# Two cross-attention layers on one core: the last batch's image values weighed by a TensorE product with a block-diagonal matrix

## The reference, cut to what matters

```python
probs_ip = jax.nn.softmax(fused, axis=-1)                 # b h s 4
probs_ip = probs_ip * spatial_mask[None, None, :, None]
ip_out = jnp.einsum('bhsn,bhnd->bhsd', probs_ip, v_ip)    # 4 image values per head
ip_out = ip_out.transpose(0, 2, 1, 3).reshape(B, S, C)
out = text_out + IP_SCALE * ip_out                        # IP_SCALE = 1
out = out @ W_out + b_out
out = out + residual
```

## Time and profile before

| | |
|---|---|
| runs | 1620.91, 1628.34, 1626.88 us, median 1626.88 |
| profiled execution | 1620.88 us, of which the span of its instructions is 1619.1 us |
| PE busy | 1521.6 us, 94% of the span |
| DVE busy | 1270.9 us, 78% |
| ACT busy | 1051.9 us, 65% |
| POOL busy | 421.7 us, 26% |
| granted TensorE clock, mean | 0.983 |

### The profile page before, as it was taken

One profiled execution on the slowest core, in us unless ns is written; L12 is line 12 of the kernel. 1 busy time (PEld: TensorE's weight loads), 2 busy tenths in 40 slices (PEclk: granted clock), 3 DMA queues, 4 the chain that ended last, 5 costly groups with the idle time before them and its releaser, 6 DMA issues.

```text
span 1619.1 us, 24966 instructions
## 1 busy us (share of the span) xinstructions
PE 1521.6 (94%) x7536; PEld 1154.4 (71%) x7536; DVE 1270.9 (78%) x3537; ACT 1051.9 (65%) x2243; POOL 421.7 (26%) x993
## 2 busy tenths in 40 slices
PE   6899999999999999999999999999999999999993
PEld 3565389999656549999856637999965654899991
DVE  2598379998779738999779945999977983799985
ACT  1598267776269737777529936777725982777760
POOL 0244022222034302322104412222302440232220
PEclk9899999999999999999999999999999999999996
DMA  9211321111411132111131123111140113111110
GB/s 300 62 45 22 107 58 21 21 21 23 127 26 43 44 95 63 25 21 17 47 103 40 36 76 101 21 21 21 19 136 16 45 37 107 16 26 21 21 18 16
DMA packets 160222, 84.50 MB, mean 52 GB/s; under 512 B 121925, under 2 KB 130901, under 8 KB 160089
## 3 DMA queue, kind: packets, MB, share of 16 engines
q1 hardware_dynamic: 157448, 77.80, 19.5%
q10 hardware_dynamic: 2640, 5.11, 0.9%
HBM read 41.78 MB, written 34.10 MB: 47 GB/s over the span
## 4 chain that ended last, share of the span: by engine, by line
PE 85%; ACT 6%; issue 3%; SPq 2%; DVE 2%; DMA 1%; DVEq 0%; ACTq 0%
PE ps_w L1029 50%; PE ps_s L1029 16%; PE ps_t L1029 12%; PE ps_b L1029 5%; ACT probs L591 3%; PE ps_b L1154 2%; ACT probsT_high L572 1%; ACT probsT L580 1%; DMA slots<-out_all 1%; DVE row_max L802 1%; SPq L373 1%; SPq L325 0%; DMA slots<-probsT_low 0%; ACT probs L677 0%; PE ps_m L1029 0%
## 5 line engine op out<-in xcount | busy, mean ns | idle before, releaser
L572 ACT ACTIVATE probsT_high<-ps_t 128x512 fp32r<-128x512 f32 x640 | 385.1, 602 | 95.9 <-PE ps_t L1029 92.7
L787 DVE TENSOR_TENSOR probsT_low<-probsT,probsT_high 128x512 fp32r<-128x512 f32 x560 | 378.9, 686 | 17.3 <-ACT probsT L580 12.0
L580 ACT ACTIVATE probsT<-ps_t 128x512 f32<-128x512 f32 x640 | 388.2, 606 | 0.0
L1029 PE MATMUL ps_w<-gram,probsT_high 128*128 128x416 f32 (+2 forms) x1280 | 383.9, 310 | 1.1 <-issue 1.1
L1029 PE MATMUL ps_w<-gram_low,probsT_high 128*128 128x384 f32 (+2 forms) x1280 | 351.5, 303 | 0.0
L606 ACT ACTIVATE probs<-ps_s,row_max 128x508 f32<-128x508 f32 x320 | 222.5, 696 | 145.9 <-DVE row_max L852 105.5
L1029 PE MATMUL ps_s<-slots 96*128 96x512 f32 x640 | 280.6, 481 | 23.9 <-DVE row_max L802 9.3
L1029 PE MATMUL ps_t<-slots 98*128 98x512 f32 x640 | 251.6, 413 | 1.1 <-ACT probsT L580 0.2
L1029 PEld LDWEIGHTS ps_w<-gram_low,probsT_high 128*128 128x128 f32 (+1 forms) x1280 | 241.9, 189 | 6.3
L1029 PE MATMUL ps_w<-gram,probsT_low 128*128 128x400 f32 (+2 forms) x1280 | 245.9, 314 | 0.0
L1029 PEld LDWEIGHTS ps_w<-gram,probsT_high 128*128 128x128 f32 (+1 forms) x1280 | 240.4, 188 | 6.1 <-issue 1.8
(11 more groups left out here) (175 smaller groups left out, 1854.1 us busy)
## 6 DMA issues: line engine op xcount, KB each, us to landing
slots<-parts SPq DMA_DIRECT2D x128, 192.0 KB, 3.4
slots<-row_max SPq DMA_DIRECT2D x640, 0.5 KB, 2.0
parts<-probsT_high SPq DMA_DIRECT2D x16, 512.0 KB, 4.2
parts<-probsT_high SPq DMA_DIRECT2D x24, 256.0 KB, 4.1
parts<-probsT_low SPq DMA_DIRECT2D x8, 512.0 KB, 3.6
parts<-x_sb SPq DMA_DIRECT2D x8, 512.0 KB, 3.9
slots<-probsT_high SPq DMA_DIRECT2D x24, 128.0 KB, 3.3
parts<-probsT_low SPq DMA_DIRECT2D x12, 256.0 KB, 3.6
```

The costliest lines, as they stand in the source:

```text
L572: nc.scalar.activation(probsT_high[1 - par][:, t, :], ps_t[:, t % 2, :], ACT.Exp, scale=scale)
L580: nc.scalar.activation(probsT[:, t, :], ps_t[:, t % 2, :], ACT.Exp, scale=scale).then_inc(pt_block[l], 1)
L787: nc.vector.tensor_tensor(probsT_low[1 - par][:, t, :], probsT[:, t, :], probsT_high[1 - par][:, t, :].bitcast(F32), ALU.subtract).then_in ...
L1029: return nc.tensor.matmul(out, lhsT, rhs, start=start, stop=stop)
```

## The change

In the last batch alone, VectorE no longer weighs the image values. It writes the text part of the heads straight to the place that is transposed, in four products (one a chunk), and releases `heads_ready` there. It then normalizes the image weights in four products of 128x80 into `fused_by_chunk`. TensorE transposes the heads as before, then these weights (four transposes, 80 rows of result), and ScalarE copies the result into `fusedT` (80 x 512). With `vip_diag`, a matrix of 80 x 320 that holds each head's 4 x 16 image values on its diagonal and zeros elsewhere, three products on TensorE give the image share of the transposed heads; VectorE adds it to `heads_outT`, in three additions; then the output products follow. `vip_diag` lies in the place of `vip_rep`: GpSimd fills it with zeros after batch 2's `heads_ready`, and SyncE loads its blocks with 20 DMAs (one a head) in place of the four broadcasts. The first three batches are otherwise as they were.

```diff
--- before.py
+++ after.py
@@ -139,6 +139,9 @@
         ip_sq = sb("ip_sq", [P, EB, IPS])
         v0_slot = [sb(f"v0_slot{p}", [P, TB, V0S], F32R) for p in range(2)]
         vip_rep = sb("vip_rep", [P, IPN, C])
+        vip_diag = vip_rep[0:HEADS * IPN, 0, :]
+        fusedT = ctx_sb[0:HEADS * IPN, 0, :]
+        fused_by_chunk = ctx_sb[:, 1, 0:HEADS * SC * IPN].rearrange("p (c n) -> p c n", c=SC)
         slots = sb("slots", [ALL_ROWS, SLOTS, 2, S], F32R)
         q_slots, k_slots = slots[:, :, 0, :], slots[:, :, 1, :]
         q_slot, k_slot = [[t[:, i, :] for i in range(SLOTS)] for t in (q_slots, k_slots)]
@@ -204,6 +207,9 @@
         high_in = sem("high_in")
         ctx_ip_in, ip_sq_in = sem("ctx_ip_in"), sem("ip_sq_in")
         ip_done, ip_in = sem("ip_done"), sem("ip_in")
+        image_done, image_in = sem("image_done"), sem("image_in")
+        diag_zero, diag_in = sem("diag_zero"), sem("diag_in")
+        fused_in, fusedT_done, fusedT_in = sem("fused_in"), sem("fusedT_done"), sem("fusedT_in")
         stored = {n: sem(f"stored_{n}") for n in scratch}
         vip_stored, vip_rep_in = sem("vip_stored"), sem("vip_rep_in")
         y_out = sem("y_out")
@@ -435,13 +441,23 @@
                     row = IPN * batch + i
                     sp.dma_start(vip_rep[:, i, :], vip_dram[row:row + 1, :].to_broadcast([P, C])).then_inc(vip_rep_in, 16)
 
+            def spread_ip_values(batch):
+                sp.wait_ge(diag_zero, 1)
+                sp.sem_inc(passed, 1)
+                for h in range(HEADS):
+                    sp.dma_start(vip_diag[IPN * h:IPN * h + IPN, D * h:D * h + D],
+                                 vip_dram[IPN * batch:IPN * batch + IPN, D * h:D * h + D]).then_inc(diag_in, 16)
+
             split_and_loaded(FIRST, 0, 0, ("k0", "q0"))
             load_biases()
             for b in range(BATCH):
                 split_and_loaded(b, b, 1, ("k1", "q1"))
                 if b == 0:
                     store_ip_values()
-                repeat_ip_values(b)
+                if b < BATCH - 1:
+                    repeat_ip_values(b)
+                else:
+                    spread_ip_values(b)
                 if b < BATCH - 1:
                     split_and_loaded(b, b + 1, 0, ("k0", "q0"))
                 else:
@@ -541,6 +557,10 @@
                     values_of(b, 1, 1)
 
                 run_heads(step1, pool, b, gram_ready)
+                if b == BATCH - 2:
+                    pool.wait_ge(heads_ready, 2 * b + 2)
+                    pool.sem_inc(passed, 1)
+                    nc.gpsimd.memset(vip_diag, 0.0).then_inc(diag_zero, 1)
                 if ahead:
                     wait_freed(pool, b, "v0i", TB - 1)
                     pool.sem_inc(passed, 1)
@@ -718,6 +738,9 @@
                     for t in range(TB):
                         v0_ip(b, t)
                 move_transposed(b, "tr1")
+                if not ahead:
+                    act.wait_ge(fusedT_done, 1)
+                    nc.scalar.activation(fusedT, ps_m[0:HEADS * IPN, :], ACT.Copy).then_inc(fusedT_in, 1)
                 if ahead:
                     fill0(step0, b + 1, b)
 
@@ -981,15 +1004,36 @@
                     .then_inc(ask_exp, 1)
                 if ahead:
                     low(b, "q0", 0)
-                nc.vector.tensor_tensor(wide[0], o1[:, :, V1:V1 + D], rz.to_broadcast([P, nd, D]), ALU.mult)
                 if ahead:
+                    nc.vector.tensor_tensor(wide[0], o1[:, :, V1:V1 + D], rz.to_broadcast([P, nd, D]), ALU.mult)
                     low(b, "k0", 1)
+                else:
+                    o4 = o1.rearrange("p (h c) w -> p h c w", c=SC)
+                    rz4 = stat[:, :, 2].rearrange("p (h c) -> p h c", c=SC)
+                    for c in range(SC):
+                        last = nc.vector.tensor_tensor(by_head[:, :, c, :], o4[:, :, c, V1:V1 + D],
+                                                       rz4[:, :, c].unsqueeze(2).to_broadcast([P, HEADS, D]), ALU.mult)
+                    last.then_inc(heads_ready, 1)
                 dve.wait_ge(exp_in, b + 1)
                 link(b, nc.vector.tensor_reduce(out=tot, in_=fused[:, :, :], axis=AX.X, op=ALU.add))
                 link(b, nc.vector.reciprocal(tot, tot))
                 tot3 = stat[:, :, 6].rearrange("p (h c) -> p h c", c=SC)
                 mask3 = mask_sb[:, :].unsqueeze(1).to_broadcast([P, HEADS, SC])
                 link(b, nc.vector.tensor_tensor(tot3, tot3, mask3, ALU.mult))
+                if not ahead:
+                    in_chunks = fused[:, :, :].rearrange("p (h c) i -> p c h i", c=SC)
+                    tot_chunks = stat[:, :, 6].rearrange("p (h c) -> p c h", c=SC)
+                    for c in range(SC):
+                        last = nc.vector.tensor_tensor(fused_by_chunk[:, c, :].rearrange("p (h i) -> p h i", i=IPN), in_chunks[:, c, :, :],
+                                                       tot_chunks[:, c, :].unsqueeze(2).to_broadcast([P, HEADS, IPN]), ALU.mult)
+                    last.then_inc(fused_in, 1)
+                    for m in range(CBN):
+                        dve.wait_ge(image_done, m + 1)
+                        wait_freed(dve, b, "tr1", m)
+                        nc.vector.tensor_tensor(heads_outT[0:CB[m], m, :], ring[m][0:CB[m], :], heads_outT[0:CB[m], m, :], ALU.add)                            .then_inc(image_in, 1)
+                    for m in range(CBN):
+                        output(b, m)
+                    return
                 link(b, nc.vector.tensor_tensor(fused[:, :, :], fused[:, :, :], tot.to_broadcast([P, nd, IPN]), ALU.mult))
                 f4 = fused[:, :, :].rearrange("p (h c) i -> p h c i", c=SC)
                 vr = vip_rep[:, :, :].rearrange("p i (h d) -> p i h d", d=D)
@@ -1010,11 +1054,7 @@
                 assert links[0] <= CHAIN_B, links[0]
                 while links[0] < CHAIN_B:
                     link(b, nc.vector.memset(dump[:, 8:9], 0.0))
-                if ahead:
-                    fill0(step0, b + 1, b)
-                else:
-                    for m in range(CBN):
-                        output(b, m)
+                fill0(step0, b + 1, b)
 
             for name, m in HIGHS[len(HIGHS1):]:
                 low(FIRST, name, m)
@@ -1320,6 +1360,21 @@
                                                    ident[:, :])
                     last.then_inc(job_done, 1)
 
+            def heads_with_image(b):
+
+                rows = HEADS * IPN
+                transposed_heads(b, "tr1", 1)
+                pe.wait_ge(fused_in, 1)
+                pe.sem_inc(passed, 1)
+                for c in range(SC):
+                    last = nc.tensor.transpose(ps_m[0:rows, P * c:P * c + P], fused_by_chunk[:, c, :], ident[:, :])
+                last.then_inc(fusedT_done, 1)
+                pe.wait_ge(fusedT_in, 1)
+                pe.wait_ge(diag_in, 16 * HEADS)
+                for m in range(CBN):
+                    mm(ring[m][0:CB[m], :], vip_diag[:, P * m:P * m + CB[m]], fusedT, True, True).then_inc(image_done, 1)
+                pe.wait_ge(image_in, CBN)
+
             def batch(b, ahead):
                 run_heads0(step0, pe, b)
                 pe.wait_ge(weights_in, WEIGHTS)
@@ -1345,8 +1400,7 @@
                     fill0(step0, b + 1, b)
                     wait_freed(pe, b, "y", CBN - 1)
                 else:
-                    transposed_heads(b, "tr1", 1)
-                    wait_freed(pe, b, "tr1", CBN - 1)
+                    heads_with_image(b)
                     by_channels(b, "y", "o1", heads_outT)
 
             queries_keys0(FIRST, 0)
```

## The result

The changed kernel takes 1615.47 us (median of four runs, 1612.34 to 1619.93) where the kernel before takes 1627.56 (four runs); the ratio is 0.9939, 95% interval 0.9921 to 0.9957: 12.1 us less by the medians, 9.9 us by the ratio (7.0 to 12.9 us by its interval, clear of noise). Forecast were 10.4 us less and 1616.5 us. Two later repetitions of the unaltered changed kernel gave ratios of 0.9933 (0.9908 to 0.9958) and 0.9940 (0.9919 to 0.9961). So the total was right.

The account below looks back on a forecast made before the run. TensorE bounds the kernel (busy 94%), but VectorE's chain bounds the last batch's tail. Saving 8.0 us up to the output products plus 2.4 in them, 10.4 us off the 1626.88 us median, gives 1616.5 us; range 1611 to 1622.

Parts of the forecast that it names:

- VectorE's chain: Last batch, up to `heads_ready`: four products take 1.69 us, and TensorE starts its transposes 14.77 us earlier.
- Weights under the transposes: VectorE normalizes image weights in four products, 1.0 us, hidden under 2.81 us of heads' transposes; cost on the path zero.
- Transposed weights and copy: After the heads' transposes: four more transposes on TensorE, 0.94 us, then ScalarE's copy of 80 x 512, 0.59 us.
- Image products: Three 512-column, 80-row products on TensorE after ScalarE's copy: 5.0 us, bounds 2.9 and 5.8.
- Pause and addition: Between image and output products: VectorE's last addition and the handing-over leave TensorE idle 0.8 us.
- Output products: Nine products at the tail's end: 8.86 us against 11.22 with the clock up, gain 2.4 us, bounds 0 and 2.4.
- I let the clock rise 4.2 us into these products: Image products: TensorE's clock returns to full 4.2 us in, middle of three earlier rises after 3.5, 3.7 and 4.85 us.
- Rival 1: Tail: clock rises only among the output products, which take 10.7 to 11.2 us; saves 7.3 to 7.8, 1619.3 us; chance 0.34.
- Rival 3: Tail: transposes do count, so the clock rises at 1590.9; 12.3 us saved, 1614.6 us; chance 0.05.
- Rival 2: SP's queue: the 20 small loads become the wait; at 2.5 us per issue, 1640 us; chance 0.03.

Follow-up runs that it names:

- experiment 1: Changed kernel plus nine unread 512-column products on TensorE in the hole between last head and transposed heads; 1609.96 us, ratio 0.9901 to the kernel before.
- experiment 11: The changed kernel again, unaltered, beside the kernel before; 1614.80 us (six runs, 1609.94 to 1621.09).
- experiment 5: The changed kernel once more, unaltered, beside the kernel before; 1613.84 us (six runs, 1606.69 to 1620.74).
- experiment 3: Changed kernel without the last batch's image share: no weight transposes, image products, copy or additions; 1606.21 us, ratio 0.9890 to the kernel before.
- experiments 4 and 10: Changed kernel with image products of 128 rows instead of 80, added rows zeros; 1612.21 us, ratio 0.9912, and 1609.04 us, ratio 0.9906.
- 7: Changed kernel with image values multiplied by output weights ahead in the hole, entering as a fourth product per output block; 1609.45 us, ratio 0.9899.
- experiment 12: Changed kernel with 60 small loads on SyncE's queue instead of 20, image products waiting for all; 1608.08 us, ratio 0.9903 to the kernel before.
- experiment 9: Changed kernel plus nine 512-column products in the hole, with 80 rows in both operands instead of 128; 1607.68 us, ratio 0.9898.

## Why the prediction came out

**VectorE's chain** (14.77 us forecast): 14.77 measured, with the four products at 1.69.

**Weights under the transposes** (1.0 us for the four, ready before the transposes end): 0.70, ready 0.84 us before. Right. At the full clock that cover is gone and 0.6 us shows (experiment 1).

**Transposed weights and copy** (0.94 and 0.59): 0.87 and 0.59. Right.

**Image products**: forecast 5.0 us, as a mean of a low and a high part. Measured 5.7 with the low clock throughout (the profile after, experiment 11) or 3.0 with the full clock throughout (experiment 5). The bounds 2.9 and 5.8 were right, the value between them occurred in no profile.

**Pause and addition** (0.8): 0.78.

**Output products**: forecast 8.86, bounds 8.86 and 11.22. Measured 8.9 when the clock is up, 13.15 and 13.0 when it isn't. Here the bound was wrong: it was taken from the kernel before, whose products ran low for 4.85 us and then at the full clock; ones that run low for 8.5 to 8.8 us cost 13.

**The step that failed** is "I let the clock rise 4.2 us into these products". In no profile did it. The premise was that some 3.5 to 4.9 us of work without a pause raise the clock. The trace of before has two more rises that fit it (at 66.32, 4.6 us into such work, and at 1226.85, 3.5 us into it), but the profile after has 8.3 us ahead of the rise at 169.04 and 8.8 ahead of that at 1609.47, so time at work alone doesn't set it. In six profiles (experiments 3, 4, 5, 7, 10, 12) it rose 2.8 to 3.8 us after the first transpose, before any product that follows. In the profile after and in experiment 11 it stayed low through all the transposes, 5.7 us of image products without a pause, and 8.5 to 8.8 us of output products. The mean over both comes near the sum: 10.4 forecast, 10.0 measured between the mean of the changed kernel's 16 runs (1615.1) and the 36 later runs of before (1625.1). In the tail alone, 12.8 us saved with the early rise and 5.6 with the late one give 9.2 if each comes half the time, which is an estimate from the eight of 16 runs with a mean clock of 0.986 or more. That the middle value was near this mean is luck: a right total over a wrong middle.

**The rivals.** Rival 1 (0.34) is the profile after in kind, at a higher price: 5.6 us saved in the tail, not 7.3 to 7.8, since the rise came later still. Rival 3 (0.05), the transposes raising the clock, is what experiment 5 shows: 26.5 us of tail, 12.8 less than before (12.3 forecast). It was given far too little, on the word of the rule named in the prediction and of one profile that seemed to agree with it. The Trainium skill, page "TensorE: Matmul & The Clock Gate", Part 4 (PE-mode transpose), says that transposes don't count towards the full clock; experiment 3, where the clock rose 3.4 us after the first transpose and before the first product, goes against it. The profile before, with its rise 8.3 us after the first transpose, was one execution; profiles of the changed kernel show both kinds. Rival 2 is out by experiment 12: the loads take 0.30 us each at the median (0.36 over the 20), half of the row that was taken.

**Open.** Why the clock sometimes rises in the transposes and sometimes only 16 us later. That 80-row products hold back a rise is consistent with the profile after and experiment 11 and with the shorter mean of experiments 4 and 10. Against it are experiment 9, which refutes its stronger form, experiment 12, which is as fast without wider products, and the 8.5 to 8.8 us of output products of up to 128 rows that followed at the low clock in those two profiles. No profile shows 128-row image products that began low.

## What to carry to other kernels

Where one engine's chain leaves TensorE idle at the very end of a kernel, moving its arithmetic to TensorE pays although TensorE is the bound elsewhere: 12.7 us of VectorE's products and sums became 3.0 to 5.7 us of products on TensorE, or 4.3 to 7.3 us with the transposes, the copy and the addition that go with them. But price each TensorE step behind a hole at both clocks, separately and for the whole stretch, and don't take a middle value from the one execution at hand: this tail was 26.5 or 33.6 us long with nothing changed. Compare stretches of the same code in both profiles first: the last head ended up to 8 us apart with nothing changed in TensorE's work ahead of it. And look for what the idle hole can take over: multiplying the output weights in ahead took 1.4 to 1.6 us off the tail, and nine products in the hole whose result nobody reads, which kept the clock up, took 7.7 us off the slower of the two tails and 0.6 off the faster.

## What the runs showed of the hardware beyond expectation

In experiment 3 the granted clock rose to 1.00 right behind twelve transposes of 128 columns in 2.8 us, with no product since the hole; in the profile after and in experiment 11 it stayed at 0.50 behind the same transposes. It can also fall while TensorE works: at 162.22 in the profile after, 1.4 us into a stretch without a pause, where the profile before kept 1.00 throughout the same code. Of 512-column products in four-byte floats at the full clock, 24 with the same weights took 20.6 us, 0.86 us apiece; the nine output products, with changing weights, took 8.9. A four-by-sixteen block of values took SyncE 0.30 us to issue at the median (0.36 in the mean of a row of 20 and of 60), less than its half-kilobyte loads (0.60).
